# Sync engine's queue around the first expert blocks: a store, a weight load and a 4 MB load change their places

## The reference

```
# part 1: a selective state space layer
h = rmsnorm(x) * norm_scale @ w_in;  xs, res = split(h);  res = silu(res)
xs = silu(causal_conv(xs, conv_w, conv_b))          # 4 taps, 512 channels
delta, B, C = split(xs @ w_xproj);  delta = softplus(delta @ w_dt + b_dt)
state = scan(exp(delta * A), delta * xs * B)        # 16 states for each channel
y = sum(state * C) + xs * D
x = layernorm(x + x + (y * res) @ w_out)
# part 2: a mixture of 8 experts, each token uses 2
n = rmsnorm(x) * norm_weight
shared = relu(n @ sw1 + sb1) @ sw2 + sb2
w, idx = top_k(sigmoid(n @ router_w.T), 2);  w = w / sum(w)
routed = sum over the 2 experts e of w_e * (relu(n @ ew1[e] + eb1[e]) @ ew2[e] + eb2[e])
out = layernorm(x + shared + routed)
```

## Time and profile before

| | us |
|---|---|
| timed runs, median of 3 | 1727.56 (1727.55 to 1731.47) |
| profiled execution | 1725.55 |
| its span, first to last instruction | 1723.5 |
| TensorE busy, share of the span | 1483.5, 86% |
| DVE busy | 1193.8, 69% |
| GpSimd busy | 952.4, 55% |
| ACT busy | 906.6, 53% |
| mean granted TensorE clock | 0.914 of 2.4 GHz |
| DMA | 252.14 MB, mean 146 GB/s |

### The profile page before, as it was taken

The page is one execution under the profiler, slowest core; times in us unless marked ns, Lnnn a source line. Parts: engine busy times, 40 slices in busy tenths (PEclk is TensorE's granted clock), DMA queues, the critical chain, the costliest instruction groups (busy, mean ns, idle before and its releaser), DMA issues.

```text
span 1723.5 us, 24541 instructions
## 1 busy us (share of the span) xinstructions
PE 1483.5 (86%) x6945; PEld 967.7 (56%) x6946; DVE 1193.8 (69%) x2113; ACT 906.6 (53%) x1778; POOL 952.4 (55%) x590
## 2 busy tenths in 40 slices
PE   7386799989989989989988769967999999999970
PEld 3131235525525525526535326767999999999960
DVE  4499999999999999999999997212333333333327
ACT  4477666777766777665786553212333333333324
POOL 1677797798798798788799884301111111111115
PEclk9697998998998998988999889888999999999995
DMA  5833653455554444534535521936555555555538
GB/s 157 220 94 86 147 135 92 119 131 123 124 127 113 124 120 123 138 96 123 135 94 131 139 67 63 302 103 237 182 179 179 180 179 178 180 180 183 181 126 264
DMA packets 136951, 252.14 MB, mean 146 GB/s; under 512 B 15313, under 2 KB 68418, under 8 KB 136754
## 3 DMA queue, kind: packets, MB, share of 16 engines
q1 hardware_dynamic: 130402, 233.49, 48.6%
q0 software_dynamic: 6480, 17.83, 2.8%
HBM read 205.76 MB, written 45.51 MB: 146 GB/s over the span
## 4 chain that ended last, share of the span: by engine, by line
PE 51%; DVE 26%; ACT 11%; issue 7%; SPq 3%; DMA 2%; POOL 0%; DVEq 0%; ACTq 0%; POOLq 0%
DVE psH L1124 16%; PE psH L1541 15%; PE psP L1552 14%; PE psP L1382 6%; DVE big L1133 6%; PE psP L1371 4%; ACT psH L960 2%; PE psA L1480 2%; PE psA L1461 2%; PE psP L1400 2%; PE psP L1445 2%; SPq L710 1%; PE psA L1471 1%; PE psP L1529 1%; DMA ew_s<-in_L_ffn_ew_dram 1%
## 5 line engine op out<-in xcount | busy, mean ns | idle before, releaser
L472 POOL TENSOR_TENSOR big<-big,B 128x2048 f32<-128x2048 f32 x128 | 578.1, 4530 | 106.1 <-PE psA L1480 51.0
L960 ACT ACTIVATE psH<-big,A_q 128x512 f32<-128x512 f32 x512 | 351.7, 691 | 146.0 <-DVE big L1133 121.5
L1133 DVE TENSOR_TENSOR big<-psH,C 128x512 f32<-128x512 f32 x512 | 350.8, 685 | 0.0
L1124 DVE TENSOR_TENSOR_SCAN psH<-psH,big 128x512 f32<-128x512 f32 x256 | 313.3, 1224 | 50.9 <-ACT psH L960 31.1
L576 POOL DMA_INDIRECT con_dram<-eo,dest x71 | 68.3, 962 | 490.8 <-ACT eo L1032 482.9
L1124 DVE TENSOR_TENSOR_SCAN psH<-psH,carry,big 128x512 f32<-128x512 f32 x256 | 331.8, 1296 | 11.0 <-ACT psH L960 11.0
L1541 PE MATMUL psH<-nTb,ew_s 128*128 128x128 f32 x2272 | 271.4, 279 | 12.9 <-DMA ew_s<-in_L_ffn_ew_dram 8.8
L1541 PEld LDWEIGHTS psH<-nTb,ew_s 128*128 128x128 f32 x2272 | 270.8, 196 | 17.1 <-issue 13.7
L1552 PE MATMUL psP<-big,hT 128*128 x1136 | 257.0, 379 | 0.7 <-DVE eb L1290 0.7
L1480 PE MATMUL psA<-big,gsum 128*32 128x512 f32 x1024 | 218.3, 661 | 44.5 <-DVE big L1133 43.4
L1261 DVE TENSOR_TENSOR hT<-psH,vecs 128x512 f32<-128x512 f32 x142 | 98.2, 692 | 196.4 <-PE psH L1541 196.4
(11 more groups left out here) (173 smaller groups left out, 1544.4 us busy)
## 6 DMA issues: line engine op xcount, KB each, us to landing
ew_s<-in_L_ffn_ew_dram SPq DMA_DIRECT2D x71, 1024.0 KB, 4.8
big<-ud_dram SPq DMA_DIRECT2D x128, 512.0 KB, 8.6
ud_dram<-ud SPq DMA_DIRECT2D x32, 512.0 KB
xb<-rows_dram SPq DMA_DIRECT2D x71, 130.0 KB, 2.1
B<-bc_dram SPq DMA_DIRECT2D x128, 64.0 KB, 5.7
C<-bc_dram SPq DMA_DIRECT2D x128, 64.0 KB, 5.6
big<-in_L_ffn_ew_dram SPq DMA_DIRECT2D x8, 1024.0 KB
big<-con_dram SPq DMA_DIRECT2D x16, 512.0 KB, 8.8
```

Source lines behind the costliest of these rows:

```text
L472: nc.gpsimd.tensor_tensor(X[:, Q % NX], rep[:, g % 2, 1], B4[:, f:f + 1, :].broadcast_to([P, NR, TC]), ALU.mult).then_inc(bx_ready, 1)
L960: nc.scalar.activation(psH[:, r, :], rep[:, g % 2, 0, r, :], ACT.Exp, scale=A_q[:, c, r, f:f + 1]).then_inc(dA_ready, 1)
L1124: nc.vector.tensor_tensor_scan(psH[:, r, :], psH[:, r, :], X[:, Q % NX, r, :], start, ALU.mult, ALU.add).then_inc(scan_done, 1)
L1133: nc.vector.tensor_tensor(X[:, Q % NX, r, :], psH[:, r, :], C4[:, f, :], ALU.mult).then_inc(hc_ready, 1)
```

## The change

Three parts, all in SP's stream, and one wait of DVE that follows from the last:

1. The store of the last tile's first half, `store_acc(NT - 1, 0)`, stands between load_up(1) and the loop of zeroings. The second half's store stays behind load_block(1).
2. `load_up(2, 0)` stands between load_block(2) and load_block(3), ahead of the waits for block 3, and not behind load_block(3).
3. The 4 MB load of `xall` is cut into 32 loads of 128 KB (128 rows of 1 KB), one at the end of each of the 32 passes of the loop. The wait for all stores (`acc_out`) stays ahead of the loop. DVE's first use of `xall` waits for 32 landings in place of one.

```
@@ -724,6 +724,7 @@
             for i in range(2):
                 load_up(i, i)
+            store_acc(NT - 1, 0)
             with sp.Fori(0, E) as e:
                 row = sp.value_load(tail_row[0:1, ds(e, 1)], min_val=0, max_val=(E - 1) * REGION + T)
                 sp.dma_start(rows_dram[ds(row, P), :], zero[:]).then_inc(zeroed, 16)
@@ -737,13 +738,13 @@
             for i in range(2):
                 load_block(i, i)
-            for h in range(2):
-                store_acc(NT - 1, h)
+            store_acc(NT - 1, 1)
             for i in range(2):
                 sp.wait_ge(T_done, i + 1)
                 sp.wait_ge(meta_done, i + 1)
                 load_block(i + 2, i)
-            load_up(2, 0)
+                if i == 0:
+                    load_up(2, 0)
             def one_pass(t):
@@ -754,9 +755,11 @@
             one_pass(0)
             sp.wait_ge(acc_out, 16 * 2 * NT)
-            sp.dma_start(xall[:], acc_dram.rearrange("(t p) d -> p t d", p=P)).then_inc(x_back, 16)
+            acc_rows = acc_dram.rearrange("(t p) d -> p t d", p=P)
+            assert NBLK // 2 - 2 == NSUBS + 1
             with sp.Fori(1, NBLK // 2 - 2) as t:
                 one_pass(t)
+                sp.dma_start(xall[:, ds(t - 1, 1)], acc_rows[:, ds(t - 1, 1)]).then_inc(x_back, 16)
             load_up(NBLK - 2, 1)
@@ -1318,7 +1321,7 @@
                 if k == 0:
-                    dve.wait_ge(x_back, 16)
+                    dve.wait_ge(x_back, 16 * NSUBS)
```

## The result

| | before | after |
|---|---|---|
| timed runs, median of 4 | 1727.97 us (1727.55 to 1731.47) | 1704.25 us (1701.90 to 1708.52) |
| profiled execution | 1725.55 us | 1701.90 us |
| its span | 1723.5 us | 1699.9 us |
| TensorE busy | 1483.5 us | 1473.8 us |
| mean granted clock | 0.914 | 0.924 |

The ratio is 0.9861 with a 95% interval of 0.9836 to 0.9886: faster by 1.4%, 23.7 us, where 17.9 us were forecast.

A forecast was written before the change was run, and what follows sets the result against it. TensorE, always busy in the loop over expert blocks, was held up by three holes ending in late SP issues. Gains 0.2 + 5.9 + 11.8 = 17.9 us, off the 1727.56 us median, gave 1709.7 us; range 1704.5 to 1716.5.

The forecast's parts named there:

- hole 1: TensorE's 8.95 us wait before rows_T(0): moving the store only changes what it waits for; gain 0.2 us.
- Hole 3: TensorE's 8.81 us wait before expert_up(5), weights queued behind the 4 MB load: goes, with its slow clock; gain 11.8 us.
- Hole 2: TensorE's 4.08 us wait for expert_up(2)'s weights: goes, with its slow clock; gain 5.9 us.
- cover of 2.6: In the loop, weights land 2.6 us before TensorE needs them, so chunk delays of 0.5 to 1.0 us stay hidden.
- Rivals B and C: B: new waits take back about 5 us, 1714.7, chance 0.13. C: chunks delay weights every pass, slower than before, 0.04.
- estimate of 2.3 us: Time per chunk by the skill's page; the load_up behind would come 2.7 us late, costing 3 us over the loop.
- shift of 2.5 to 2.9 us: At the moved store, SP's wait and issue delay the zeroings and first row loads by this much.
- slow steps: SP's 0.70 us register instructions around the first zeroings, 2.4 us lost; taken as paid again behind the new store wait.
- rival A: SP's slow register instructions are paid during the new store wait: total gain 20.3 us, 1707.3 us; chance 0.20.
- middle value: The 0.2 us taken for the store's move, between the ends of 2.6 and -0.5 us.

The follow-up runs named there:

- experiment 3: Only the 32 loads of 128 KB in the loop, against the kernel before: 1715.19 us, ratio 0.9942.
- experiment 2: Only load_up(2) moved ahead of load_block(3), against the kernel before: 1721.07 us, ratio 0.9970.
- experiments 15 to 17: Kernel before, unedited, one execution each for three more profiles: 1721.72, 1721.99 and 1726.46 us.
- 5 and 11: Changed kernel again, no edit, against the kernel before: 1707.11 us (ratio 0.9903) and 1706.28 us (ratio 0.9912).
- experiments 12 and 13: Both kernels on one chip, no edit: 12 the kernel before, 1725.16 us; 13 the changed kernel, 1703.95 us, ratio 0.9880.
- experiments 1 to 4: Against the kernel before: store move alone, load_up(2) alone, chunks alone, the last two together: 1724.34, 1721.07, 1715.19, 1708.69 us; kernel before 1726.90 us.
- experiment 10: Changed kernel with the loop of eight zeroings written out, same order: 1699.77 us, ratio 0.9881 to the kernel before.

## Why the prediction was wrong

It was wrong by its range and by its first term; the mechanisms of holes 2 and 3 were as forecast, and that of hole 1 in part. The two spans differ by 23.6 us, 5.7 more than the 17.9 forecast: 3.0 of these are A and B, 2.4 are hole 1 with its clock (C), and 0.3 are D.

**Hole 3, 11.8 us.** Right. D falls by 11.2 us in experiment 3 and its time by 11.7. The issue of a chunk is 0.35 us of SP and lands in 2.1; the load_up behind it is issued 0.57 us later in its pass (2.12 us behind the row load instead of 1.55), inside the cover of 2.6. Rivals B and C did not come. The rule of the Trainium skill ("DMA: Bandwidth & Descriptors", section "Rules for kernel authors") that for maximum bandwidth a DMA should have 1 MiB or more pointed the wrong way here, where bandwidth was not the limit: the 32 small ones cost nothing that TensorE sees, four of 1 MiB cost 3 us. The fixed 2.0 us that the prediction took from the same page of the Trainium skill (section "Anatomy of one DMA") are given there for the path of the DMAs that GpSimd issues, and the chunks are SP's; the estimate of 2.3 us is near the 2.1 measured all the same, but the load_up behind a chunk landed in 4.9 us, so these 2.0 us were not paid by the load behind.

**Hole 2, 5.9 us.** Right: 5.8 us in experiment 2, no idle time, 3.73 us for expert_up(2). load_up(2) went out 1.8 us after the start of DVE's first addition and 0.02 us after that of the second, so as its own wait let it.

**Hole 1, 0.2 us.** The step that failed. That the wait would change its name from the additions to the rows is what the trace shows, but the shift of 2.5 to 2.9 us was mis-sized: it took the slow steps as bound to the place in SP's program, to be paid again behind the new wait. They go with the time of GpSimd's scatters, so SP spends a part of them waiting at the store, and in the first pair the shift was 1.2 us and the gain 2.6 us. That is the gain that rival A gave, though its time, 1707.3 us, was not met either. Of these 2.6 us 2.0 are the shorter hole (8.95 to 6.97) and 0.6 a clock that rose earlier (8.61 instead of 9.19 us for expert_up(0) and (1)), a part that I had left out for this hole although I counted it for the other two. Over all profiles with slow steps the term is 2.2 us. In executions without them it is -0.2 us, near the value taken, but by luck: the old hole was 5.0 to 5.9 us there and not 8.95, and from the end of load_up(1) to row load 0 SP needed 18.2 to 18.8 us with the store moved against 14.8 to 15.6, a shift of 3.4 us, more than forecast. I had read one profile and could not see that there are both. The rule of the Trainium skill ("Runtime: NRT & Kernel Launch", section "Instruction fetch mechanics") that I cited for the middle value, on the fetch behind a taken branch, has nothing on its side: the slow steps came with the loop written out as well, and in the kernel before the first of them, 0.70 us at 1108.89, lies inside load_up(1), ahead of the loop.

**The scatter.** The remaining 3.0 us of the first pair, A and B, are no effect of the change. The point A alone lies between 1054.4 and 1065.1 us in 19 profiles of the same code, and the time of an execution goes with the granted clock: among the kernel before's runs of experiments 1 to 4 those at a mean clock of 0.910 to 0.912 took 1727.2 to 1729.3 us and the one at 0.924 took 1719.1. I gave 2 us for this beside the cases, from three runs that lay 3.9 us apart. The four comparisons of the change give ratios of 0.9861, 0.9903, 0.9912 and 0.9880, so 14 to 24 us. By the profiles from A on and without the chance part of B the change is worth 17.4 us without slow steps (659.1 before, the mean of experiments 15 to 17, against 641.7, that of 5 and 11) and 19.6 with them (661.7 against 642.1, from the first pair and experiments 12 and 13, the 2.7 us taken off). The forecast of 17.9 lies between the two; the range was too narrow at its lower end for a difference of medians of three and four runs.

Not settled: why some executions have the slow steps, and whether they are there at all in executions that are not recorded. The chip does not decide it: one chip showed both kinds for the kernel before (experiment 12, and 15 to 17). The comparisons whose profiles have the slow steps gained 23.7 and 22.0 us, those without 15.7 and 13.7; the profiles explain 2.2 us of that distance, and the rest stays open.

## What to carry to other kernels

A large load that nobody needs soon should not stand in the queue ahead of small loads that somebody needs: here 4 MB cost 11.8 us in one queue, 3 us as four pieces, 1.0 us from another engine's queue (where the loads beside it took up to 8.6 us instead of 4.8, which their cover hid), and nothing as 32 pieces between the others. Work out for the load behind it how much later it may land; that cover tells how large a piece may be.
When a wait is moved to the front of a queue, look at what ends the hole next: here it was the issues behind it, and writing out their loop (3.5 us) was worth more than moving the wait. A hole short enough to leave the clock at its upper level pays twice, as that of 2.2 us did in experiment 10.
Before a sum of small terms is set against one profile, ask how much the same code differs between two profiles.

## What the runs showed of the hardware that was not expected

- The register load of a zeroing took 0.51 us in most passes of its loop and 0.27 us written out. That is no matter of the loop alone: in the loop over blocks the register loads took 0.27 us, and so did some of the first passes of the zeroings (experiment 15). What makes the difference is open.
- Register instructions of 0.03 to 0.15 us took 0.7 us each while GpSimd's last scatters were under way, in 9 of the 19 profiles and not in the others, with the same instructions; the 9 are those whose trace lacks the landings of the scatters.
- A second queue shields the small loads in part: beside 4 MB from ScalarE's queue SP's 1 MB loads took 6.1 to 8.6 us instead of 4.8, against 16 us behind the same 4 MB in SP's own.
- The same 64 matmuls of expert_up(0) and (1) took 7.31 us behind a hole of 2.23 us (experiment 10), and 8.61 and 9.19 us behind holes of 6.97 and 8.95 us; the granted clock over them was 1.00, 0.84 and 0.78.
